# A fused model on one core: the gates of the experts moved ahead of the up matmul, in fp32, and spread by DMAs from DRAM

## The chip, the cores and the metric

The kernel runs on one core of one Trainium2 chip. The metric is the device time of one execution in microseconds, as the median of several runs. A core has TensorE (PE), VectorE (DVE), ScalarE (ACT), GpSimd (POOL) and SyncE (SP), each with its own queue of instructions; they order one another by semaphores, and SP and ScalarE issue DMAs.

## The reference

The whole model is computed in one launch: a mix of four geometric features into 64 channels, a state-space network of four layers, a mixture of experts, an attention and an LSTM, each with a layer norm ahead and a residual. There are 64 sequences of T = 96 tokens with 64 channels. The change is in the mixture of experts, with E = 16 experts, hidden width F = 128, the best K = 2 taken:

```python
gate_logits = x @ gate_w + gate_b
topk_vals, topk_idx = jax.lax.top_k(gate_logits, K)
topk_w = jax.nn.softmax(topk_vals, axis=-1)
h = jax.nn.relu(jnp.einsum('bsh,ehf->bsef', x, w1) + b1)
expert_out = jnp.einsum('bsef,efh->bseh', h, w2) + b2
sel = jnp.take_along_axis(expert_out, topk_idx[:, :, :, None], axis=2)
moe = jnp.sum(topk_w[..., None] * sel, axis=2)
y = x + moe
```

x is here a layer norm of h over its 64 channels, without scale and shift, so its channels sum to zero. A layer norm of y, with gamma and beta, follows. Everything is fp32.

## The kernel before

Every engine has its instructions written out in a block of its own, with explicit semaphores (`S("name")`); the order in the code is the order on the engine. Semaphores of the expert stage: `m_z` up, `m_r` relu, `m_g` gate spread, `m_h` product, `m_d` down, `m_mo` result out of PSUM.

The 6144 tokens stand as 12 groups `q` of 512 (NQ = 12). Every group passes all 16 experts, each weighted by its gate, which is zero for 14 of them. Experts go in pairs: the even one on partitions 0 to 63 of the 64-row operands, the odd one on 64 to 127. XD holds x with the channels on partitions, twice. There are 96 pairs, in six blocks `i` of 16 pairs `P` (two groups). For each pair:

- `up` (PE, line 1334): two fp32 matmuls of W1f with 512 tokens of XD into PSUM banks 0 to 3
- `weigh` (PE, line 1341): two bf16 matmuls of a 0/1 matrix `sel` with GP, the gates cut in three bf16 pieces, which give each expert's gate on all 128 partitions, in banks 4 and 5
- ACT, line 591: relu with the bias b1T into Rb; DVE, line 935: product of Rb and the gates in PSUM into Hb; one each for either expert
- `down` (PE, line 1326): two fp32 matmuls of w2s with Hb, summed over the experts in bank 6; ahead of a group's first, three bf16 matmuls add b2 times the gates (line 1324)

TensorE's order is up, weigh, down of the pair before. In the first block VectorE also computes the second part of the gates (`gate(1, k)`, 24 steps). In the other blocks the layer norm of the block before stands between the products (`settle`, in the pairs that the table SETTLE names), with GpSimd's powers and scaling, ScalarE's squares and copies, and TensorE's transposes (`sums_out`, `norm_out`). The gates are computed token-major on VectorE, turned by TensorE (`gates_turn`, line 1283) and copied out by ScalarE (`gates_out`, line 568). `xs_pe`, `xs_act` and `xs_dve` fill XD ahead of that. At the start of the program SP issues all loads in one order; GpSimd builds constants, `sel` among them, and prepares b2.

## Time and profile before

| | |
|---|---|
| median of 3 runs | 954.13 us (952.63 to 955.64) |
| the profiled execution | 950.02 us, span 947.5 us |
| PE busy | 772.4 us (82%) |
| DVE busy | 586.2 us (62%) |
| ACT busy | 393.7 us (42%) |
| POOL busy | 250.6 us (26%) |
| expert stage | 234.4 to about 488 us |
| DMA over the span | 10.21 MB, 11 GB/s mean |

Times of rows are from one profiled execution. In a timeline a row is: start in us, length in us, engine, line, operation, output<-inputs, shape, count; in brackets the idle time of the engine ahead of it and who ended it. In a group of instructions the two numbers after the bar are busy us and mean ns of one. An fp32 matmul of the program is recorded as two instructions, and two of them run side by side on the halves of the array. Lines are those of the kernel before.

### The profile page before, as it was taken

The numbers are of one execution on the slowest core, as the hardware profiler recorded it, in microseconds if no ns is written. First come the engines' busy times: TensorE is split into PE (matmuls) and PEld (weight loads), VectorE is DVE, ScalarE is ACT, GpSimd is POOL, SyncE is SP. The second block draws the span as 40 slices with busy tenths as digits, with TensorE's granted clock in tenths as the row PEclk, the third lists the DMA queues.
The fourth block names the chain that finished last, engine by engine and source line by source line (L and its number), as shares of the span: only waits on it lengthen the run. The fifth ranks groups of instructions, "written<-read, shape, count | busy, mean of one in ns | idle before, by whom it ended". The sixth has DMA issues, their size and how long they took to land.

```text
span 947.5 us, 17575 instructions
## 1 busy us (share of the span) xinstructions
PE 772.4 (82%) x6745; PEld 441.9 (47%) x6745; DVE 586.2 (62%) x1243; ACT 393.7 (42%) x791; POOL 250.6 (26%) x211
## 2 busy tenths in 40 slices
PE   3788888536999999999985777888999688888875
PEld 2675556425232222222223444565767555555554
DVE  4847655697766676676655655476776645545543
ACT  2233434233465565656541142344545233333332
POOL 8675555581001110202110302122233311001100
PEclk9988898755999999999986677799999955555555
DMA  9700000000000000000000000000000000000000
GB/s 190 126 8 1 1 1 1 1 0 1 1 1 1 1 1 1 1 1 1 1 0 1 1 1 1 2 1 2 1 1 2 1 7 10 10 10 10 10 10 12
DMA packets 23838, 10.21 MB, mean 11 GB/s; under 512 B 17414, under 2 KB 23574, under 8 KB 23766
## 3 DMA queue, kind: packets, MB, share of 16 engines
q1 hardware_dynamic: 22678, 8.92, 5.1%
q8 instruction: 54, 0.88, 0.4%
q10 hardware_dynamic: 1088, 0.26, 0.2%
q14 instruction: 18, 0.15, 0.1%
HBM read 7.60 MB, written 1.57 MB: 10 GB/s over the span
## 4 chain that ended last, share of the span: by engine, by line
PE 30%; DVE 11%; ACT 6%; issue 4%; POOL 1%; DVEq 0%; ACTq 0%; POOLq 0%
PE PS L1543 6%; PE PS L1398 3%; PE PS L1377 3%; PE PS L1447 3%; PE PS L1458 2%; PE PS L1419 2%; ACT LS L679 2%; ACT LS L675 2%; PE PS L1429 2%; DVE LS L1057 2%; DVE LS L1049 2%; DVE LS L1055 2%; PE PS L1326 1%; PE PS L1334 1%; DVE am L992 1%
## 5 line engine op out<-in xcount | busy, mean ns | idle before, releaser
L935 DVE TENSOR_TENSOR XC<-PS,Y 128x512 f32<-128x512 f32 x192 | 124.8, 686 | 80.9 <-ACT Y L591 80.7
L591 ACT ACTIVATE Y<-PS,b1T 128x512 f32<-128x512 f32 x192 | 121.2, 683 | 96.0 <-PE PS L1334 95.8
L1334 PE MATMUL PS<-XD,W1f 64*128 64x512 f32 x384 | 109.3, 646 | 1.6 <-ACT UF L568 1.6
L1543 PE MATMUL PS<-LS,V 64*64 64x32 f32 x1140 | 80.7, 294 | 34.7 <-DVE LS L1057 32.8
L1326 PE MATMUL PS<-XC,w2s 128*64 128x512 f32 x384 | 104.4, 622 | 1.9 <-DVE XC L935 1.9
L1543 PEld LDWEIGHTS PS<-LS,V 64*64 64x64 f32 x1140 | 67.9, 215 | 68.4 <-DVE LS L1057 66.7
L463 POOL TENSOR_TENSOR st<-st,mhalf 128x8 f32<-128x8 f32 x12 | 19.6, 1636 | 250.4 <-DVE st L918 250.4
L1334 PEld LDWEIGHTS PS<-XD,W1f 64*128 64x128 f32 x384 | 29.3, 186 | 66.4 <-ACT Y L591 50.3
L675 ACT ACTIVATE LS<-PS 128x64 f32<-128x64 f32 x96 | 21.4, 223 | 87.3 <-PE PS L1543 86.6
L1049 DVE SCALAR_TENSOR_TENSOR LS<-LS 128x32 f32<-128x32 f32 x96 | 19.6, 205 | 60.2 <-ACT LS L675 60.2
L1377 PE MATMUL PS<-BIG,MMs 64*128 64x512 f32 x96 | 37.0, 853 | 19.6 <-ACT EX L615 6.8
L175 POOL TENSOR_TENSOR st<-st,mhalf 128x8 f32<-128x8 f32 x24 | 39.3, 1637 | 47.0 <-DVE st L768 47.0
L1533 PE MATMUL PS<-XD,U 65*64 65x128 f32 x288 | 48.6, 439 | 0.8 <-ACT XD L669 0.8
L1341 PE MATMUL PS<-UF,sel 48*128 48x512 bf16 x192 | 37.2, 381 | 9.9 <-DVE XC L935 9.7
L494 POOL TENSOR_TENSOR st<-st,mhalf 128x8 f32<-128x8 f32 x6 | 9.8, 1636 | 126.8 <-DVE st L1041 126.8
L1178 PE MATMUL PS<-ident,UT 128*128 128x128 f32 x120 | 24.5, 339 | 21.1 <-POOL UT L177 21.0
L1447 PE MATMUL PS<-Y,UT 32*64 32x128 f32 (+2 forms) x768 | 35.7, 277 | 5.7 <-ACT XC L627 3.0
L992 DVE TENSOR_REDUCE am<-PS 128x8 f32<-128x768 f32 (+2 forms) x28 | 29.5, 1053 | 16.5 <-PE PS L1401 12.6
L482 POOL TENSOR_TENSOR Y<-Y,am 128x768 f32<-128x768 f32 (+1 forms) x10 | 16.4, 1644 | 85.0 <-DVE am L981 42.9
L1341 PEld LDWEIGHTS PS<-UF,sel 48*128 48x128 bf16 x192 | 9.4, 93 | 61.6 <-DVE XC L935 59.2
L1326 PEld LDWEIGHTS PS<-XC,w2s 128*64 128x64 f32 x384 | 19.0, 134 | 40.6 <-issue 37.8
L1057 DVE SCALAR_TENSOR_TENSOR LS<-LS 128x32 f32<-128x32 f32 x96 | 18.4, 192 | 28.3 <-ACT LS L679 28.3
(243 smaller groups left out, 1525.2 us busy)
## 6 DMA issues: line engine op xcount, KB each, us to landing
BIG<-in_x SPq DMA_DIRECT2D x8, 512.0 KB, 12.0
out<-X SPq DMA_DIRECT2D x48, 32.0 KB, 2.0
W1f<-in_L_ffn_w SPq DMA_DIRECT2D x2, 512.0 KB, 6.2
H<-in_txt SPq DMA_DIRECT2D x2, 256.0 KB, 12.3
w2s<-in_L_ffn_w SPq DMA_DIRECT2D x1, 512.0 KB, 6.1
BB<-in_L_attn_Bm ACTq DMA_DIRECT2D x2, 64.0 KB, 6.2
bds<-in_L_attn_Dm SPq DMA_DIRECT2D x2, 64.0 KB, 2.7
XD<-in_L_attn_Wq SPq DMA_DIRECT2D x1, 128.0 KB, 2.9
```

The costliest lines, as they stand in the source:

```text
L175: pool.tensor_tensor(st[:, 3, sj], st[:, 2, sj], mhalf[:, 0:KC * 2], ALU.pow).then_inc(S("s_r"), 1)
L591: act.activation(Rb[:, e % 4, :], PS[:, e % 4, :], ACT.Relu, bias=b1T[:, e:e + 1]).then_inc(S("m_r"), 1)
L675: act.activation(Tb[:, u % 2, 0:2 * HN], PS[:, 2 + par, 2 * HN * s:2 * HN * (s + 1)], ACT.Tanh).then_inc(S("l_t"), 1)
L935: dve.tensor_tensor(Hb[:, e % 4, :], PS[:, 4 + e % 2, :], Rb[:, e % 4, :], ALU.mult).then_inc(S("m_h"), 1)
L992: dve.tensor_reduce(stat_a(x, 0), scores(UNITS[x]), AX_X, ALU.max).then_inc(S("a_mx"), 1)
L1326: pe.matmul(PS[64 * (e % 2):64 * (e % 2) + 64, 6, :], w2s[:, e, :], Hb[:, e % 4, :], start=False, stop=(p == E - 2)).then_inc(S("m_d"), 1)
L1334: pe.matmul(PS[:, e % 4, :], W1f[r, e, :], XD[r, q * 512:(q + 1) * 512], start=True, stop=True).then_inc(S("m_z"), 1)
L1341: pe.matmul(PS[:, 4 + e % 2, :], sel[r, e, :], GP[r, q * 512:(q + 1) * 512], start=True, stop=True).then_inc(S("m_g"), 1)
L1377: pe.matmul(PS[:, 6 + h, :], MMs[p, half, :, :].rearrange("p a d -> p (a d)"), XAb[p, b0:b0 + GA, RB * r:RB * r + RB], start=True, stop=Tr ...
L1447: mm = pe.matmul(PS[64 * a:64 * a + 64, 4 + (JOBS[u] + k) % 2, x * 128:(x + 1) * 128], XT[p, u % 2, x, :], PT[p, u % 2, a, x, :], start=Tr ...
L1533: mm = pe.matmul(dst[64 * h:64 * h + 64], U3[:, g, :], xt[:, :, h, :], start=(g != 1), stop=(k == 0), skip_group_check=True)
L1543: mm = pe.matmul(PS[r, b, o:o + HN], V3[r, g, :], HB[r, (t - 1) % 4, :], start=False, stop=True, skip_group_check=True)
```

## The change

The gate now multiplies the input of an expert instead of its hidden values. This is right because relu(g z) = g relu(z) for g of zero or more, and g x W1 + g b1 = g (x W1 + b1). So that b1 needs no step of its own, row 0 of XD is set to one (scale 0 and bias 1 on that partition, by `zo`), row 0 of W1f becomes b1, and W1's row 0 is subtracted from the other rows (the channels of x sum to zero). The gate weights are treated likewise. The gates stay in fp32: turned by one transpose for each 16 columns (`gates_turn`), copied out (GT), written to a DRAM tensor gd, and read back by two DMAs for each pair, each of which reads one row of 512 gates for 64 partitions, into one of NS = 6 slots GB. VectorE multiplies XD by GB into Rb (`weigh`). The relu of a pair is ScalarE's for the even expert and VectorE's for the odd one. The gate matmuls (`weigh` on TensorE) go, and so do the b2 matmuls of each group: b2 times the gates is one fp32 matmul for each 1024 tokens (`bias_out`), added to X by VectorE (`bias_in`).

```diff
+        gw0 = sb("gw0", [128, E])
+        zo = sb("zo", [128, 2])
+        gd = nc.dram_tensor("gd", [NC, E, CH * 128], F32)
...
+        G2 = UT[:, :, :, :].rearrange("p k h d -> p (k h d)")[:, 0:NC * 128].rearrange("p (c e m) -> p c e m", c=NC, e=E)
+        GT = EX[:, 0:NC * 128].rearrange("p (c t) -> p c t", c=NC)
+        b2d = EX[:, 2048:2560].rearrange("p (m d) -> p m d", m=CH)
+        W10 = EX[:, 0:E * F].rearrange("p (e f) -> p e f", e=E)
+        NS = 6
+        GB = UF[:, :, :].rearrange("p k c -> p (k c)").rearrange("p (n c) -> p n c", n=NS)
...
-                    act.activation(XDp()[0:64, 4 * c:4 * c + 4, a, :], bank4(4 + c % 2)[64 * a:64 * a + 64], ACT.Copy).then_inc(S("xs_h"), 1)
...
+                    act.activation(XDp()[0:64, 4 * c:4 * c + 4, a, :], bank4(4 + c % 2)[64 * a:64 * a + 64], ACT.Identity,
+                                   bias=zo[0:64, 1:2], scale=zo[0:64, 0:1]).then_inc(S("xs_h"), 1)
...
-                    dve.tensor_copy(XDp()[64:128, 4 * c:4 * c + 4, a, :], bank4(4 + c % 2)[64 * a:64 * a + 64]).then_inc(S("xs_l"), 1)
...
+                    dve.tensor_scalar(XDp()[64:128, 4 * c:4 * c + 4, a, :], bank4(4 + c % 2)[64 * a:64 * a + 64], zo[64:128, 0:1], zo[64:128, 1:2],
+                                      ALU.mult, ALU.add).then_inc(S("xs_l"), 1)
...
-            sp.dma_start(b1s[:, :], b1).then_inc(S("ld_moe"), 16)
+            sp.dma_start(W10, w1[:, 0, :].rearrange("(a e) f -> a e f", a=1).to_broadcast([128, E, F])).then_inc(S("ld_w1"), 16)
+            sp.dma_start(gw0[:, :], gate_w[0:1, :].to_broadcast([128, E])).then_inc(S("ld_w1"), 16)
             sp.dma_start(w2s[:, :, :], w2.rearrange("e f h -> f e h")).then_inc(S("ld_moe"), 16)
-            for g in range(3):
-                sp.dma_start(b2f[E * g:E * g + E, 0, :], b2).then_inc(S("ld_moe"), 16)
+            sp.wait_ge(S("b2z"), 1)
+            for m in range(CH):
+                sp.dma_start(b2d[m:128:CH, m, :], b2).then_inc(S("ld_moe"), 16)
...
+            sp.wait_ge(S("w1c"), 2)
+            for h in range(2):
+                sp.dma_start(W1f[64 * h:64 * h + 1, :, :], b1.rearrange("(a e) f -> a e f", a=1)).then_inc(S("ld_b1"), 16)
+            def gates_write(c):
+                sp.wait_ge(S("g_t"), c + 1)
+                sp.dma_start(gd[c, :, :].rearrange("e t -> (e t)").rearrange("(p t) -> p t", p=128), GT[:, c, :]).then_inc(S("gdw"), 16)
+            def gates_spread(n):
+                if n >= NS:
+                    sp.wait_ge(S("m_x"), n - NS + 1)
+                q, p = n // (E // 2), n % (E // 2)
+                for h in range(2):
+                    sp.dma_start(GB[64 * h:64 * h + 64, n % NS, :],
+                                 gd[q // 2, 2 * p + h:2 * p + h + 1, q % 2 * 512:q % 2 * 512 + 512].to_broadcast([64, 512])).then_inc(S("gb%d" % (n % NS)), 16)
+            for n in range(NQ * E // 2):
+                if n == 0:
+                    gates_write(0)
+                    gates_write(1)
+                    sp.wait_ge(S("gdw"), 32)
+                if n == 22:
+                    for c in range(2, NC):
+                        gates_write(c)
+                if n == 2 * E:
+                    sp.wait_ge(S("gdw"), 16 * NC)
+                gates_spread(n)
...
-            seq(pool.memset(sel[:, :, :], 0.0), "sel")
-            for g in range(3):
-                for r in range(2):
-                    seq(pool.affine_select(out=sel[:, :, :], in_=sel[:, :, :], compare_op=ALU.not_equal, fill=1.0,
-                                       base=-E * g - 64 * r, pattern=[[-1, E], [0, F]], channel_multiplier=1), "sel")
+            seq(pool.memset(b2d, 0.0), "b2z")
+            for k in range(2):
+                seq(pool.memset(zo[:, k:k + 1], 1.0 - k), "zo")
+                for h in range(2):
+                    seq(pool.memset(zo[64 * h:64 * h + 1, k:k + 1], 1.0 * k), "zo")
...
-            pool.wait_ge(S("ld_moe"), 16 * 8)
-            seq(pool.memset(b2p[:, :, D:2 * D], 0.0), "b2z")
-            for i in range(3):
-                seq(pool.tensor_copy(b2p[:, i, 0:D], b2f[:, i % 2, :]), "b2c")
-                if i < 2:
-                    seq(pool.tensor_tensor(b2f[:, (i + 1) % 2, :], b2f[:, i % 2, :], b2p[:, i, 0:D], ALU.subtract), "b2c")
+            pool.wait_ge(S("ld_w1"), 16 * 6)
+            seq(pool.tensor_tensor(W1f[:, :, :], W1f[:, :, :], W10, ALU.subtract), "w1c")
+            seq(pool.tensor_tensor(GWs[:, :], GWs[:, :], gw0[:, :], ALU.subtract), "w1c")
...
-                act.wait_ge(S("gp_tp"), c + 1)
-                act.activation(GP[0:64 + 3 * E, c * CW:(c + 1) * CW], PSb[0:64 + 3 * E, gate_bank(c), :], ACT.Copy).then_inc(S("gp"), 1)
+                act.wait_ge(S("g_tp"), c + 1)
+                act.activation(GT[:, c, :], PS[:, gate_bank(c), 0:128], ACT.Copy).then_inc(S("g_t"), 1)
...
-                        act.activation(Rb[:, e % 4, :], PS[:, e % 4, :], ACT.Relu, bias=b1T[:, e:e + 1]).then_inc(S("m_r"), 1)
...
+                    n = i * E + P
+                    act.wait_ge(S("m_z"), n + 1)
+                    if n >= 2:
+                        act.wait_ge(S("m_d"), n - 1)
+                    act.activation(Hb[:, n % 2 * 2, :], PS[:, n % 2 * 2, :], ACT.Relu).then_inc(S("m_h"), 1)
...
-                    op = dve.tensor_tensor(LG, K1, K2, ALU.add)
-                elif k in (19, 21, 23):
-                    op = dve.tensor_copy(gp[:, :, (k - 19) // 2, :], (LG, SC, K1)[(k - 19) // 2])
-                elif k == 20:
-                    op = dve.tensor_tensor(SC, LG, gp[:, :, 0, :], ALU.subtract)
                 else:
-                    op = dve.tensor_tensor(K1, SC, gp[:, :, 1, :], ALU.subtract)
+                    ca, cb = a // CH, b // CH
+                    op = dve.tensor_tensor(G2[:, ca:cb, :, :].rearrange("p c e m -> p c m e"), K1.rearrange("p (c m) e -> p c m e", m=CH),
+                                           K2.rearrange("p (c m) e -> p c m e", m=CH), ALU.add)
...
+            def weigh(n):
+                q, p = n // (E // 2), n % (E // 2)
+                dve.wait_ge(S("gb%d" % (n % NS)), 32 * (n // NS + 1))
+                if n >= 4:
+                    dve.wait_ge(S("m_z"), n - 3)
+                dve.tensor_tensor(Rb[:, n % 4, :], XD[:, q * 512:(q + 1) * 512], GB[:, n % NS, :], ALU.mult).then_inc(S("m_x"), 1)
+            def bias_in(c):
+                dve.wait_ge(S("b2x"), c + 1)
+                xc = X[:, c * CH:(c + 1) * CH, :]
+                dve.tensor_tensor(xc, PS[:, gate_bank(c), :].rearrange("p (m d) -> p m d", d=D), xc, ALU.add).then_inc(S("b2a"), 1)
+            def relu(n):
+                dve.wait_ge(S("m_z"), n + 1)
+                if n >= 2:
+                    dve.wait_ge(S("m_d"), n - 1)
+                dve.tensor_scalar(Hb[:, n % 2 * 2 + 1, :], PS[:, n % 2 * 2 + 1, :], 0.0, None, ALU.max).then_inc(S("m_h1"), 1)
             def experts(i, first=False):
-                for qq in range(2):
-                    for e in range(E):
-                        n = i * 2 * E + qq * E + e
-                        dve.wait_ge(S("m_r"), n + 5)
-                        dve.wait_ge(S("m_g"), n + 1)
-                        dve.wait_ge(S("m_d"), n + 1)
-                        dve.tensor_tensor(Hb[:, e % 4, :], PS[:, 4 + e % 2, :], Rb[:, e % 4, :], ALU.mult).then_inc(S("m_h"), 1)
-                        step = qq * E + e
-                        if first and step < 12:
-                            gate(1, step + 1)
-                        if first and 14 <= step <= GOPS:
-                            gate(1, step - 1)
-                        if not first and e % 2:
-                            for k in SETTLE.get(step // 2, ()):
-                                settle(i - 1, k)
+                for P in range(E):
+                    n = i * E + P
+                    relu(n)
+                    if n + 2 < NQ * E // 2:
+                        weigh(n + 2)
+                    if first:
+                        if P == 0:
+                            bias_in(0)
+                            bias_in(1)
+                        for k in ((1, 2), (3, 4), (5, 6), (7, 8), (9, 10), (11, 12), (), (13, 14, 15), (16, 17), (18,))[P] if P < 10 else ():
+                            gate(1, k)
+                        if P >= 12:
+                            bias_in(P - 10)
...
+                pe.transpose(PS[:, gate_bank(c), 0:128], G2[:, c, :, :].rearrange("p e m -> p (e m)"), ident[:, :]).then_inc(S("g_tp"), 1)
+            def bias_out(c):
+                pe.wait_ge(S("g_t"), c + 1)
+                pe.matmul(PS[:, gate_bank(c), :], GT[:, c, :], b2d.rearrange("p m d -> p (m d)"), start=True, stop=True).then_inc(S("b2x"), 1)
...
-                if p == 0:
-                    pe.wait_ge(S("m_mo"), q + 2)
-                    for g in range(3):
-                        pe.matmul(PS[:, 6, :], b2p[:, g, :], GP[0:3 * E, q * 512:(q + 1) * 512], start=(g == 0), stop=False)
-                for e in (p, p + 1):
-                    pe.matmul(PS[64 * (e % 2):64 * (e % 2) + 64, 6, :], w2s[:, e, :], Hb[:, e % 4, :],
-                              start=False, stop=(p == E - 2)).then_inc(S("m_d"), 1)
...
+                p = n % (E // 2)
+                pe.wait_ge(S("m_x"), n + 1)
+                if n >= 2:
+                    pe.wait_ge(S("m_h"), n - 1)
+                    pe.wait_ge(S("m_h1"), n - 1)
+                for h in range(2):
+                    r = slice(64 * h, 64 * h + 64)
+                    mm = pe.matmul(PS[:, n % 2 * 2 + h, :], W1f[r, 2 * p + h, :], Rb[r, n % 4, :], start=True, stop=True)
+                mm.then_inc(S("m_z"), 1)
...
-            def weigh(n):
-                q, p = n // E, n % E
-                pe.wait_ge(S("m_h"), n + 4)
-                for e in (p, p + 1):
-                    r = slice(64 * (e % 2), 64 * (e % 2) + 3 * E)
-                    pe.matmul(PS[:, 4 + e % 2, :], sel[r, e, :], GP[r, q * 512:(q + 1) * 512], start=True, stop=True).then_inc(S("m_g"), 1)
...
                 up(n)
-                weigh(n)
                 if n:
-                    down(n - 2)
-                if i == 0 and P >= 12:
-                    if P == 12:
+                    down(n - 1)
+                if i == 0 and P >= 10:
+                    if P == 10:
                         pe.wait_ge(S("gchain"), gates_done(1, GOPS))
-                    gates_turn(P - 10)
+                    if P > 11:
+                        bias_out(P - 10)
+                    if P > 10 and P < 15:
+                        gates_turn(P - 9)
```

How the rows move. In each fence is what stands on the engine, before or after; XC is Hb, Y is Rb (or, in GpSimd's and norm rows, another part of the same buffers), UF is GP before and GB after, EX is GT.

TensorE in the second block before, where a group of tokens begins and then the transposes of `sums_out`:

```order
L1334 MATMUL PS<-XD,W1f 128x512 x2
L1341 MATMUL PS<-UF,sel 128x512 x2
L1324 MATMUL PS<-UF,b2p 128x512 x3
L1326 MATMUL PS<-XC,w2s 64x512 x2
L1334 MATMUL PS<-XD,W1f 128x512 x2
L1341 MATMUL PS<-UF,sel 128x512 x2
L1326 MATMUL PS<-XC,w2s 64x512 x2
L1308 MATMUL PS<-ident,BIG 128x128 x4
```

The same place after:

```order
L1383 MATMUL PS<-Y,W1f 128x512 x2
L1372 MATMUL PS<-XC,w2s 64x512 x2
L1383 MATMUL PS<-Y,W1f 128x512 x2
L1372 MATMUL PS<-XC,w2s 64x512 x2
L1354 MATMUL PS<-ident,BIG 128x128 x4
```

The rows L1341 and L1324 are gone; up (now L1383) reads Rb, and down (now L1372) follows it directly.

TensorE ahead of the first pair before:

```order
L1259 MATMUL PS<-GWs,XD 128x16 x16
L1269 MATMUL PS<-W3T 64x64 x8
L1274 MATMUL PS<-Wus,W3T 64x64 x8
L1283 MATMUL PS<-identb,UT 64x128 x32
L1334 MATMUL PS<-XD,W1f 128x512 x2
L1341 MATMUL PS<-UF,sel 128x512 x2
L1334 MATMUL PS<-XD,W1f 128x512 x2
```

And after:

```order
L1309 MATMUL PS<-GWs,XD 128x16 x16
L1319 MATMUL PS<-W3T 64x64 x8
L1324 MATMUL PS<-Wus,W3T 64x64 x8
L1330 MATMUL PS<-ident,UT 128x128 x2
L1334 MATMUL PS<-EX 128x512 x2
L1383 MATMUL PS<-Y,W1f 128x512 x4
L1372 MATMUL PS<-XC,w2s 64x512 x2
```

The 32 bf16 transposes of the first two chunks are two fp32 ones, with two b2 matmuls (L1334) behind them, and up now also waits for VectorE's product.

VectorE at the end of a block and the start of the next, before (L935 is the product, L923 the copy of the turned result):

```order
L915 TENSOR_REDUCE st<-Y 128x8
L918 TENSOR_SCALAR st<-st 128x8
L935 TENSOR_TENSOR XC<-PS,Y 128x512 x6
L923 TENSOR_SCALAR BIG<-PS 64x4x2x64 x2
L935 TENSOR_TENSOR XC<-PS,Y 128x512 x6
L897 TENSOR_TENSOR Y<-PS,X 128x256
L894 TENSOR_TENSOR Y<-PS,Y 128x256
```

And after (L973 is the relu of the odd expert, L962 the product of x and gates two pairs ahead):

```order
L944 TENSOR_REDUCE st<-Y 128x8
L947 TENSOR_SCALAR st<-st 128x8
L973 TENSOR_SCALAR XC<-PS 128x512
L962 TENSOR_TENSOR Y<-XD,UF 128x512
L973 TENSOR_SCALAR XC<-PS 128x512
L962 TENSOR_TENSOR Y<-XD,UF 128x512
L973 TENSOR_SCALAR XC<-PS 128x512
L962 TENSOR_TENSOR Y<-XD,UF 128x512
L952 TENSOR_SCALAR BIG<-PS 64x4x2x64 x2
L973 TENSOR_SCALAR XC<-PS 128x512
L962 TENSOR_TENSOR Y<-XD,UF 128x512
```

Two products a pair have become one relu and one product. SP's queue, which before had nothing between the load of beta and the stores of the output, has after it:

```order
L394 DMA bet<-in_L_ffn_beta 128x64
L399 DMA W1f<-in_L_ffn_b 1x2048 x2
L403 DMA gd<-EX 128x128 x2
L410 DMA UF<-gd 64x512 x44
L403 DMA gd<-EX 128x128 x4
L410 DMA UF<-gd 64x512 x148
```

The first row is beta's load, the second b1's; then come the gates of two chunks of 1024 tokens to DRAM, and the 192 loads of gates, with the other four chunks' stores ahead of the 45th.

## Rows read from the trace of the kernel before

**Rows 1.** Busy time by stretch; last: granted clock, DMA share, GB/s.

```profile
207.00:234.40 27.40, 18.54 (x176) 16.36 (x176) 21.54 (x42) 9.25 (x16) 9.47 (x4) 0.53 0.00 1
...
234.40:278.65 44.25, 41.32 (x226) 12.37 (x227) 31.20 (x55) 23.91 (x37) 0.00 (x0) 0.96 0.00 1
...
426.86:468.73 41.87, 40.00 (x180) 11.21 (x178) 28.81 (x48) 24.49 (x39) 6.62 (x6) 1.00 0.00 1
```

**Rows 2.** Groups of the block 426.86 to 468.73, costliest first.

```profile
L935 DVE TENSOR_TENSOR XC<-PS,Y 128x512 f32<-128x512 f32 x33 | 21.3, 686 | 12.6 <-ACT Y L591 12.6
...
L591 ACT ACTIVATE Y<-PS,b1T 128x512 f32<-128x512 f32 x33 | 20.9, 683 | 15.8 <-PE PS L1334 15.7
...
L1341 PE MATMUL PS<-UF,sel 48*128 48x512 bf16 x32 | 6.2, 379 | 1.9 <-DVE XC L935 1.9
...
L923 DVE TENSOR_SCALAR BIG<-PS 64x512 f32<-64x512 f32 x2 | 2.1, 1044 | 0.1
```

**Rows 3.** Timeline of TensorE in that stage: start, length, engine, line, operation.

```profile
420.00 1.13 PE L1334 MATMUL PS<-XD,W1f 64*128 64x512 f32 x4
420.97 0.38 PE L1341 MATMUL PS<-UF,sel 48*128 48x512 bf16 x2
421.28 1.08 PE L1326 MATMUL PS<-XC,w2s 128*64 128x512 f32 x4
422.29 1.13 PE L1334 MATMUL PS<-XD,W1f 64*128 64x512 f32 x4
...
426.86 1.13 PE L1334 MATMUL PS<-XD,W1f 64*128 64x512 f32 x4
...
428.05 0.81 PE L1324 MATMUL PS<-UF,b2p 48*128 48x512 bf16 x3
...
429.79 1.13 PE L1334 MATMUL PS<-XD,W1f 64*128 64x512 f32 x4
...
441.26 0.66 PE L1316 MATMUL PS<-ident,Y 128*128 128x128 f32 x4
441.84 1.13 PE L1334 MATMUL PS<-XD,W1f 64*128 64x512 f32 x4
```

**Rows 4.** Timeline of all engines before the first expert pair.

```profile
224.77 0.88 DVE L844 TENSOR_TENSOR Y<-Y,gs 128x256 f32<-128x256 f32 x2
...
231.46 0.27 ACT L561 ACTIVATE MMs<-PS 128x128 f32<-128x128 f32 x1
...
231.75 0.38 ACT L564 ACTIVATE NPt<-PS 64x256 f32<-64x256 f32 x1
...
232.15 1.94 ACT L568 ACTIVATE UF<-PS 112x1024 bf16<-112x1024 bf16 x2
...
234.42 1.13 PE L1334 MATMUL PS<-XD,W1f 64*128 64x512 f32 x4 [1.59 <-ACT UF L568]
```

**Rows 5.** DMA issues: KB each, median us from issue to landing.

```profile
XD<-in_L_attn_Wq SPq DMA_DIRECT2D x1, 128.0 KB, 2.9
...
out<-X SPq DMA_DIRECT2D x48, 32.0 KB, 2.0
...
gam<-in_L_ffn_gamma SPq DMA_DIRECT2D x1, 32.0 KB, 3.5
```

**Rows 6.** Timeline of SP's queue: the issue of one of them.

```profile
38.93 0.52 SPq L376 DMA_DIRECT2D XD<-in_L_attn_Wq  x1
```

**Rows 7.** Busy time by stretch, while x, Wk and then gamma, beta load.

```profile
7.00:12.00 5.00, 1.54 (x12) 1.31 (x12) 0.06 (x1) 1.00 (x2) 4.71 (x3) 1.00 1.14 211
...
41.80:42.00 0.20, 0.00 (x0) 0.00 (x0) 0.20 (x2) 0.08 (x1) 0.00 (x0) 1.00 1.06 369
...
52.40:53.40 1.00, 0.45 (x3) 0.04 (x1) 0.94 (x3) 0.74 (x2) 0.92 (x2) 0.50 0.08 22
```

**Rows 8.** Timeline of GpSimd ahead of the first layer.

```profile
60.86 6.72 POOL L453 TENSOR_TENSOR H<-H,boutr 128x3072 f32<-128x3072 f32 x1
...
79.94 1.67 POOL L175 TENSOR_TENSOR st<-st,mhalf 128x8 f32<-128x8 f32 x1 [12.36 <-DVE st L768]
```

## What I predict, and why

> **What bounds the kernel now.** I read the busy time by stretch first [rows 1]. The expert stage runs from 234.4 to about 488 us. In the block of 16 pairs from 426.86 to 468.73, which I take for all five behind the first, TensorE is busy 40.0 of 41.9 us at a granted clock of 1.00 (the 2.4 GHz level), VectorE 28.8, ScalarE 24.5, and the DMA engines do nothing. So TensorE sets this stage; a change is worth here what it takes off TensorE's row of work, as long as the others stay below it.
>
> The groups of the block say what the other engines do [rows 2]: ScalarE's relu 683 ns and VectorE's product 686 ns, 32 or 33 of each, TensorE's gate matmuls 379 ns, and only 1.9 us of the block is TensorE waiting for VectorE. TensorE's rows in order of time [rows 3] give the price of each step from start to start. Up matmuls start at 420.00, gate matmuls at 420.97, down matmuls at 421.28, the next up matmuls at 422.29. A pair is 0.97 + 0.31 + 1.01 = 2.29 us. The three b2 matmuls stretch a pair from 2.29 to 429.79 - 426.86 = 2.93, so 0.64 us, and four transposes take 0.58 (441.26 to 441.84). A block is then 16 x 2.29 + 2 x 0.64 + 3 x 0.58 = 39.7 us; the 2.2 us that are left of 41.87 are stalls.
>
> **The expert blocks.** The change takes the 192 gate matmuls (`weigh` on TensorE) and the 36 b2 matmuls away. What stays per pair is up and down: 0.97 + 1.01 = 1.98 us. The trace never shows up followed directly by down. At the least the gain is a third of the 0.64 us that three b2 matmuls of the same length cost, 0.21 (2.08 per pair), if the turn from up to down costs as much as the two turns do now; at the most it is 0.38, the length of a gate matmul (1.91). I take 0.31, since 0.97 is also what up takes where its successor is ready. A block: 16 x 1.98 + 3 x 0.58 + stalls. Of the 2.2 us of stalls I keep a third, 0.7, because a late VectorE step has now a slack that it has not today: relu of pair n is ready 1.13 + 0.69 = 1.8 us after up(n) starts, and down(n), behind up(n+1), is due at 1.98 + 0.97 = 2.95. That gives 34.1 against 41.87, so 7.8 less, five times: **-38.8 us**. With all 2.2 kept it is -31.
>
> VectorE covers this. Per pair it has a relu of the odd expert from PSUM and a product of two SBUF tiles. Neither stands in the trace; the nearest is the product from PSUM, 0.69 us, of which two take 1.29 in a row, so 0.60 each from start to start. A block is 16 x 1.20 + 7.5 (28.8 less 21.3, the layer norm steps) = 26.7 of 34.1 us. ScalarE has one relu a pair in place of two, and is no candidate. If the cover were gone (each operation at 0.9 us) VectorE would need 36 us a block, and set the pace there.
>
> **The first block.** It takes 44.25 us now. VectorE still has the second part of the gates in it: 13 or so long operations, two per pair, so 4 x 0.60 = 2.4 us in six or seven pairs in place of 1.98, and two additions of the b2 product in pair 0. 31.7 + about 3.7 for VectorE + four b2 matmuls of 128x512 at about 1.0 (nearest: a down pair, 1.01) + four turns at 0.15 to 0.3 = 40.3: **-4.0 us**.
>
> **The start of the stage.** Now the last of TensorE's results before it leaves ScalarE at 232.13, two evictions of 0.97 follow, and up starts at 234.42 [rows 4]. After: two products (0.88) move behind the last x copy, so ScalarE is free at 231.3. Two evictions of 128x128 at 0.27 end at 231.8. Then two things are new and stand on the path: the gates are written to DRAM, and only then read back. A store of 32 KB lands 2.0 us after issue, a load of 64 rows of 2 KB (Wq) 2.9, and its issue takes the queue 0.52 [rows 5, 6]. 231.8 + 0.1 + 2.0 = 233.9; + 0.52 + 2.9 = 237.4; product 0.69 and two handovers: up at 238.2, **+3.8 us**. The granted clock is 0.53 ahead of the stage and 0.96 in its first block [rows 1]: TensorE enters it at the lower level either way, so the longer wait gets no term of its own. The Trainium skill (DMA: Bandwidth & Descriptors, Bandwidth) has about 2.0 us plus bytes over 436 GB/s for one DMA, 2.3 us for these 128 KB where the trace has 2.9; by it the term would be +3.2.
>
> **The spread itself.** Each pair needs two DMAs of 128 KB, 96 pairs, all reading one row of 2 KB 64 times. SP: 2 x 0.52 = 1.04 us of issue in 2.13 us a pair, six pairs ahead; covered. The transfer: 262 KB in 2.13 us is 123 GB/s. How fast can it go? [rows 7] Loads of different pieces of 1 KB (x) with a full queue: 211 GB/s. Rows of 2 KB (Wk): 369 GB/s in the 0.2 us in which they pass. But the two broadcasts of the trace, gamma and beta, 256 B read by 128 partitions each, crawl: 22 GB/s, flat for over 2 us, at an 8% share of the engines. So the engines are not short of anything; the one place that all read from is. That is the number on which this prediction hangs. If what limits is the 256 B piece, a row of 2 KB is eight such places: 8 x 22 = 176 GB/s, 1.49 us a pair, hidden below 2.13. If the whole row is one such place, it is 22 GB/s. I take the first, since distinct pieces have run at 211 and 369 in this trace and only identical ones at 22; the traces do not show a row of several pieces read by all.
>
> **Before the stage.** W10 is a broadcast of 1 MB in the load queue, over 16 rows of 512 B, 5 us at 211 GB/s. GpSimd gets a subtraction of 128x2048, 2048/3072 of the 6.72 us that the addition of 128x3072 takes, 4.5 us, and that addition is queued behind it; it ends now at 67.6, and GpSimd is next wanted at 79.94 [rows 8]. 12.4 us of slack hide 4.5 and a queue that ends some 5 us later: 0. At 22 GB/s W10 takes 48 us, the loads of the LSTM weights behind it arrive near 93, and with 13 us of GpSimd's work the layers would start at 106: +26. The x copies with a scale and a bias in place of plain ones I take at the same time.
>
> **Sum.** Against the profiled execution's own 950.02 us (span 947.5): -38.8 - 4.0 + 3.8 = -39.0, 911. The median of the three runs, 954.13, is 4.1 above it, and that is what a median is compared with: 915.
>
> **The rivals.**
> 1. *The source of the spread is the bound, and the kernel gets slower.* All 16 engines read the same row; the 22 GB/s row speaks for it, the 8% share too, the 369 GB/s against. Below 100 GB/s (262 KB in today's 2.62 us a pair) it decides. With four places per row, 88 GB/s: 2.98 us a pair, 286 us in place of 254 plus the start: 950 + 32 + 4 = 986, chance 0.12; that is the version on the slower side by a few per cent. With one or two, 22 or 44 GB/s: 11.9 or 5.96 a pair, 1144 or 572 us in place of 254: 1845 or 1270, chance 0.13.
> 2. *The spread reaches half of the 211 GB/s.* 105 GB/s, 2.49 us a pair, 239 in place of 254: about 940, and with a late start no change. Chance 0.12. The Trainium skill (DMA: Bandwidth & Descriptors, Latency and other measured facts) reports streams that walk through HBM in step at one large power-of-two pitch at 103 where others had 214 GB/s, and infers aliasing of channels; readers of one row are in step by construction. That halving of 211 is this rival; the flat 22 here is worse than the page's case.
> 3. *VectorE or the handovers set the pace* and most of the stalls stay. 26.7 of 34.1 us speaks against, the doubled steps at a block's end (two of 1.04 us beside 1.2) for it. About 925. Chance 0.13, counted within the forecast's 0.63, in whose range it lies.
>
> **How the numbers follow.** Forecast 0.63, own range 903 to 937: 1.91 or 2.08 us a pair is -7 or +10, stalls kept +8, start +-2. Rival 2 0.12, rival 1 0.12 and 0.13. From 903 to 990 leaves out the 0.13 and a few hundredths below. Faster by over 0.3% (about what a measurement here can tell from none): 0.63 and half of rival 2, 0.69; within 0.3%: 0.05; slower: 0.26.
>
> **What would show it.** Right: up starts 1.98 us apart in most pairs of a block, no wait for UF's transfers after the first, DMA near 123 GB/s through the stage, up(0) near 238, blocks of 34 us, everything before 200 us in place. Wrong: VectorE's products wait for DMAs each pair (the spacing then gives the rate of the spread: 2.98 is 88 GB/s); or up to down takes over 1.07; or VectorE late in each pair; or the first layer starts after 80 us.

## The result and the profile after

The kernel after takes 923.27 us (median, 921.92 to 927.37); the kernel before, run beside it, 953.38. The ratio is 0.968 (0.963 to 0.973; it holds a fifth execution of after, 917.70): 30 us faster, with a forecast of 915 and a range of 903 to 990. The profiled execution of after is the longest of its four, 927.37 (span 925.4).

The stage first, by the busy time in three stretches that answer to [rows 1]: ahead of the first pair, its block, and a later block.

```profile
215.80:243.29 27.49, 18.25 (x130) 13.78 (x131) 17.71 (x29) 8.18 (x15) 5.50 (x1) 0.54 0.09 25
243.29:283.83 40.54, 38.69 (x136) 9.95 (x137) 33.69 (x56) 11.49 (x22) 0.00 (x0) 0.96 0.45 141
354.93:390.59 35.66, 35.04 (x142) 9.29 (x140) 29.31 (x48) 14.02 (x23) 6.95 (x5) 1.00 0.35 118
```

A block takes 35.66 us where it took 41.87, and TensorE is busy 35.04 of them: it still sets the stage. The DMA engines, idle before, now move 118 GB/s at a 0.35 share. The groups of that last block answer to [rows 2]:

```profile
L1383 PE MATMUL PS<-Y,W1f 64*128 64x512 f32 x64 | 18.1, 641 | 0.0
L1372 PE MATMUL PS<-XC,w2s 128*64 128x512 f32 x66 | 17.9, 616 | 0.2 <-DVE XC L973 0.2
L962 DVE TENSOR_TENSOR Y<-XD,UF 128x512 f32<-128x512 f32 x17 | 12.2, 721 | 0.0
L973 DVE TENSOR_SCALAR XC<-PS 128x512 f32<-128x512 f32 x16 | 11.0, 690 | 4.4 <-PE PS L1383 4.3
L630 ACT ACTIVATE XC<-PS 128x512 f32<-128x512 f32 x16 | 9.6, 597 | 19.2 <-PE PS L1383 19.2
```

TensorE waits 0.2 us for VectorE, and VectorE's product has no wait for its DMA. TensorE's timeline at the end of the block before it answers to [rows 3]:

```profile
347.61 1.13 PE L1383 MATMUL PS<-Y,W1f 64*128 64x512 f32 x4
348.67 1.08 PE L1372 MATMUL PS<-XC,w2s 128*64 128x512 f32 x4
349.68 1.13 PE L1383 MATMUL PS<-Y,W1f 64*128 64x512 f32 x4
...
352.27 0.66 PE L1362 MATMUL PS<-ident,Y 128*128 128x128 f32 x4 [0.46 <-POOL Y L505]
352.86 1.13 PE L1383 MATMUL PS<-Y,W1f 64*128 64x512 f32 x4
```

Up to down is 1.06 us, down to up 1.01: a pair is 2.07 us. The start of the stage, all engines, answers to [rows 4]:

```profile
235.52 0.69 PE L1330 MATMUL PS<-ident,UT 128*128 128x128 f32 x2
235.62 0.28 ACT L597 ACTIVATE MMs<-PS 128x128 f32<-128x128 f32 x1 [6.17 <-PE PS L1324]
...
236.75 0.45 ACT L604 ACTIVATE EX<-PS 128x128 f32<-128x128 f32 x2
237.05 0.83 SPq L403 DMA_DIRECT2D gd<-EX  x2
...
239.10 6.86 SPq L410 DMA_DIRECT2D UF<-gd  x11
242.46 0.69 DVE L962 TENSOR_TENSOR Y<-XD,UF 128x512 f32<-128x512 f32 x1 [7.62 <-DMA UF<-gd]
243.29 1.13 PE L1383 MATMUL PS<-Y,W1f 64*128 64x512 f32 x4 [2.37 <-DVE Y L962]
```

The gates leave ScalarE at 237.20 and the first pair starts at 243.29, 6.1 us later. Next, GpSimd and VectorE at the start of the layers, which answer to [rows 8]:

```profile
66.45 0.25 POOL L481 TENSOR_SCALAR b<-b 128x12 f32<-128x12 f32 x1 [12.03 <-DMA V<-in_L_ffn_V_o]
...
68.45 4.52 POOL L483 TENSOR_TENSOR W1f<-W1f,EX 128x2048 f32<-128x2048 f32 x1
...
73.34 6.66 POOL L488 TENSOR_TENSOR H<-H,boutr 128x3072 f32<-128x3072 f32 x1
83.98 1.67 POOL L176 TENSOR_TENSOR st<-st,mhalf 128x8 f32<-128x8 f32 x1 [3.98 <-DVE st L804]
```

```profile
73.53 7.03 DVE L813 TENSOR_TENSOR Y<-Y,UT 128x512 f32<-128x512 f32 x1 [3.36 <-ACT Y L577]
...
81.92 0.68 DVE L813 TENSOR_TENSOR Y<-Y,UT 128x512 f32<-128x512 f32 x1
```

GpSimd's first power of the layers comes at 83.98 in place of 79.94. The row to look at is VectorE's: one product of 128x512 takes 7.03 us where the next of its kind takes 0.68, and it ends 0.56 us after GpSimd's addition (80.00). TensorE was early there (its matmuls of L1217 began at 67.90, those of the same step before the change, L1165, at 70.18), so more than the 4.0 us was lost.

Why GpSimd's work starts so late stands in SP's queue: the landing of W10, the issue of the eight b2 loads, and the last load of the queue, after and then before.

```profile
EX<-in_L_ffn_w SPq DMA_DIRECT2D x1, 1024.0 KB, 14.9
```

```profile
40.97 11.65 SPq L382 DMA_DIRECT2D EX<-in_L_ffn_b  x8
...
66.04 0.43 SPq L394 DMA_DIRECT2D bet<-in_L_ffn_beta  x1
```

```profile
51.01 0.43 SPq L385 DMA_DIRECT2D bet<-in_L_ffn_beta  x1
```

From the traces of before and after: 4.0 us lost ahead of the layers, 4.8 from there to the first pair, 34.6 gained between the first pair and the first attention queries (255.85 to 221.24). The rest, whose code did not change, took 457.2 before and 460.9 here. In the other executions profiled below it took 452.5 to 457.2, so differences of single spans under 5 us say nothing; stages are compared instead. The runs below were made in three series, each beside runs of the kernel before (median 952.85, 953.51 and 954.31 us).

### The profile page after: what moved, and what is told of

Same layout as the page of the kernel before. It is cut to its first block, busy times and chain, and to the rows that moved or that the text cites. A ratio compares the mean times of both kernels' runs of the same rounds, so it can differ in the third digit from the quotient of the medians.

```text
span 925.4 us, 17120 instructions
## 1 busy us (share of the span) xinstructions
PE 754.5 (82%) x6438; PEld 435.8 (47%) x6438; DVE 591.8 (64%) x1236; ACT 328.9 (36%) x695; POOL 234.2 (25%) x207
## 4 chain that ended last, share of the span: by engine, by line
PE 46%; DVE 29%; ACT 8%; issue 7%; POOL 7%; DMA 1%; ACTq 0%; SPq 0%; DVEq 0%; POOLq 0%
PE PS L1583 6%; PE PS L1383 5%; PE PS L1372 5%; PE PS L1438 4%; PE PS L1487 3%; PE PS L1417 3%; PE PS L1498 3%; ACT LS L717 2%; PE PS L1459 2%; ACT LS L713 2%; DVE Y L962 2%; POOL st L499 2%; PE PS L1469 2%; DVE XC L819 2%; DVE LS L1109 2%
## 5 line engine op out<-in xcount | busy, mean ns | idle before, releaser
L1383 PE MATMUL PS<-Y,W1f 64*128 64x512 f32 x384 | 109.3, 646 | 2.8 <-DVE Y L962 2.8
L1372 PE MATMUL PS<-XC,w2s 128*64 128x512 f32 x384 | 104.0, 619 | 2.8 <-DVE XC L973 2.0
L630 ACT ACTIVATE XC<-PS 128x512 f32<-128x512 f32 x96 | 57.3, 597 | 124.8 <-PE PS L1383 124.7
L973 DVE TENSOR_SCALAR XC<-PS 128x512 f32<-128x512 f32 x96 | 66.2, 689 | 27.3 <-PE PS L1383 27.0
L962 DVE TENSOR_TENSOR Y<-XD,UF 128x512 f32<-128x512 f32 x96 | 68.2, 710 | 8.6 <-DMA UF<-gd 8.6
L1383 PEld LDWEIGHTS PS<-Y,W1f 64*128 64x128 f32 x384 | 29.1, 186 | 70.5 <-issue 49.0
L1372 PEld LDWEIGHTS PS<-XC,w2s 128*64 128x64 f32 x384 | 19.4, 135 | 76.9 <-issue 72.2
L1417 PE MATMUL PS<-BIG,MMs 64*128 64x512 f32 x96 | 34.6, 802 | 17.8 <-ACT EX L653 6.0
L1487 PE MATMUL PS<-Y,UT 32*64 32x128 f32 (+2 forms) x768 | 38.1, 295 | 5.9 <-ACT XC L665 3.1
L1487 PEld LDWEIGHTS PS<-Y,UT 32*64 32x64 f32 (+2 forms) x768 | 30.1, 144 | 8.4 <-ACT XC L665 4.4
## 6 DMA issues: line engine op xcount, KB each, us to landing
EX<-in_L_ffn_w SPq DMA_DIRECT2D x1, 1024.0 KB, 14.9
```

What stands on the lines that cost most here:

```text
L630: act.activation(Hb[:, n % 2 * 2, :], PS[:, n % 2 * 2, :], ACT.Relu).then_inc(S("m_h"), 1)
L962: dve.tensor_tensor(Rb[:, n % 4, :], XD[:, q * 512:(q + 1) * 512], GB[:, n % NS, :], ALU.mult).then_inc(S("m_x"), 1)
L973: dve.tensor_scalar(Hb[:, n % 2 * 2 + 1, :], PS[:, n % 2 * 2 + 1, :], 0.0, None, ALU.max).then_inc(S("m_h1"), 1)
L1372: mm = pe.matmul(PS[64 * h:64 * h + 64, 6, :], w2s[:, 2 * p + h, :], Hb[:, n % 2 * 2 + h, :], start=(p == 0), stop=(p == E // 2 - 1))
L1383: mm = pe.matmul(PS[:, n % 2 * 2 + h, :], W1f[r, 2 * p + h, :], Rb[r, n % 4, :], start=True, stop=True)
L1417: pe.matmul(PS[:, 6 + h, :], MMs[p, half, :, :].rearrange("p a d -> p (a d)"), XAb[p, b0:b0 + GA, RB * r:RB * r + RB], start=True, stop=Tr ...
```

## The experiments

**1. GpSimd's work off the start of the layers.** Why does one product take 7 us? The first run moves only the subtraction:

```diff
-            pool.wait_ge(S("ld_w1"), 16 * 6)
-            seq(pool.tensor_tensor(W1f[:, :, :], W1f[:, :, :], W10, ALU.subtract), "w1c")
-            seq(pool.tensor_tensor(GWs[:, :], GWs[:, :], gw0[:, :], ALU.subtract), "w1c")
...
                 for j in range(NJ):
                     ssm_scale(pool, l, j)
+            pool.wait_ge(S("ld_w1"), 16 * 6)
+            seq(pool.tensor_tensor(W1f[:, :, :], W1f[:, :, :], W10, ALU.subtract), "w1c")
+            seq(pool.tensor_tensor(GWs[:, :], GWs[:, :], gw0[:, :], ALU.subtract), "w1c")
```

> GpSimd's subtraction of W10 from W1f moves behind the four layers; the loads stay as they are. Theory (GpSimd holds VectorE): VectorE's first product of the layers, 7.03 us long in the kernel after beside GpSimd's addition of 128x3072 (73.34 to 80.00), was started at 73.53 and could not run until that addition ended. Here the addition starts at about 68.5 and ends at 75.1, so the product ends at about 75.7, and GpSimd's first power of the layers starts at about 78.6 in place of 83.98: 5.4 us less, 918 against 923. The subtraction costs nothing in its new place, since GpSimd idles 12.5 us between the layers and the layer norm. Rival (the 7.03 us were something else, such as late data or one slow instruction): the product stays near 7 us wherever GpSimd's addition ends, and the time stays at 923. The Trainium skill (SBUF - State Buffer, practical consequences) says that a VectorE instruction with two SBUF inputs and a GpSimd one that reads SBUF lock each other out for a whole instruction; by it the theory holds.

Measured: 914.76 us (913.21 to 919.61), ratio to before 0.961 (0.954 to 0.967). GpSimd, then VectorE:

```profile
67.53 6.68 POOL L485 TENSOR_TENSOR H<-H,boutr 128x3072 f32<-128x3072 f32 x1
78.18 1.67 POOL L176 TENSOR_TENSOR st<-st,mhalf 128x8 f32<-128x8 f32 x1 [3.98 <-DVE st L804]
```

```profile
71.92 2.83 DVE L813 TENSOR_TENSOR Y<-Y,UT 128x512 f32<-128x512 f32 x1 [3.36 <-ACT Y L577]
```

The addition ends at 74.21, the product at 74.75: again 0.54 us behind it, whatever its own start. So the product's length is set by the end of GpSimd's operation, and the rival falls. The first power comes at 78.18, 5.8 us sooner than in the kernel after.

That it takes two operands from SBUF is seen in the second profile of the kernel after (experiment 8). There GpSimd subtracts from 70.01 to 74.52 and adds from 75.22 to 81.88. VectorE beside it:

```profile
71.85 3.21 DVE L813 TENSOR_TENSOR Y<-Y,UT 128x512 f32<-128x512 f32 x1 [3.36 <-ACT Y L577]
75.09 0.69 DVE L817 TENSOR_REDUCE st<-Y 128x8 f32<-128x512 f32 x1
75.81 6.61 DVE L819 SCALAR_TENSOR_TENSOR XC<-st,Y 128x512 f32<-128x512 f32 x1
```

The two operations with two SBUF operands end 0.54 us behind the subtraction and behind the addition. The reduction between them, with one, takes its 0.69 us, 0.56 of it beside the addition. The Trainium skill (SBUF — State Buffer, Who interferes with whom) says that a VectorE instruction with two SBUF inputs and a GpSimd one that reads SBUF exclude each other for the whole instruction. The rows of GpSimd's additions and subtractions agree. Its power of 128x8 does not: in the kernel after, a product of VectorE ran from 339.00 in 0.68 us inside the power's 338.50 to 340.14 (the spans of GpSimd's instructions are rough).

The second run also moves the loads of W10, gw0 and b2d behind all others.

```diff
-            sp.dma_start(W10, w1[:, 0, :].rearrange("(a e) f -> a e f", a=1).to_broadcast([128, E, F])).then_inc(S("ld_w1"), 16)
...
             for t, v, n in ((gbr, gate_b, E), (gam, gamma, D), (bet, beta, D)):
                 sp.dma_start(t[:, :], v.rearrange("(a n) -> a n", a=1).to_broadcast([128, n])).then_inc(S("ld_moe"), 16)
+            sp.dma_start(W10, w1[:, 0, :].rearrange("(a e) f -> a e f", a=1).to_broadcast([128, E, F])).then_inc(S("ld_w1"), 16)
...
```

> As the run before it, and the loads of W10, gw0 and of the eight b2 pieces are issued behind all others. Theory: GpSimd no longer waits for the LSTM weights until 66.45 (they land near 53, as before the change), its addition of 128x3072 ends before 62, the product takes 0.69 us, and GpSimd's first power starts at 77.7, 6.3 us less than after and 2.3 less than in the kernel before: 917 against 923. Rival (TensorE or VectorE are late themselves ahead of the layers): no more than 4 us come back, since 4.0 is what the layers start later than in the kernel before.

Measured: 914.99 us (912.5 to 917.83), ratio 0.960 (0.954 to 0.966). The addition runs from 56.01 to 62.73, the product takes 0.69, the first power comes at 76.68 and the first pair at 235.44 (237.78 in the run before it). So 7.3 us come back at the layers, 5.8 of them without moving a load; the 1.5 us between the two runs do not show in their medians. Beside their own runs of the kernel before, these two save 38 us, where the kernel after saved 30. That is 8 us more and within the spread of the medians of the 5.8 and 7.3 of the traces.

**2. How fast can the gates be spread?** This was the number on which the forecast hung. The gates are loaded twice, the second time into unused places, and the product waits for both.

```diff
                     sp.dma_start(GB[64 * h:64 * h + 64, n % NS, :],
...
+                    sp.dma_start(G9[n % NS][64 * h:64 * h + 64, :],
+                                 gd[q // 2, 2 * p + h:2 * p + h + 1, q % 2 * 512:q % 2 * 512 + 512].to_broadcast([64, 512])).then_inc(S("gb%d" % (n % NS)), 16)
```

> Each load of gates is issued twice, the second into unused places, and the product waits for both: 524 KB for each pair, 253 GB/s at 2.07 us a pair; SP issues four DMAs a pair, about 4 x 0.45 = 1.8 us. Theory A (one row read by 64 partitions is no special source, the engines give over 250 GB/s): the time grows by less than 5 us, blocks stay near 35.7. Theory B (the source row is a hot place and gives 8 x 22 = 176 GB/s): 2.98 us a pair, 96 x 0.91 = 87 us more, about 1010. Theory C (somewhere between, the 211 GB/s of the x loads): 2.48 us a pair, 40 us more, about 963. DMA GB/s in the stage gives the ceiling in B and C.

Measured: 958.19 us (954.14 to 961.73), ratio 1.004 (1.001 to 1.007): nearest to theory C. But SP's rows and the stretch 340 to 400 us point to another limit than the transfer:

```profile
342.34 0.60 SPq L413 DMA_DIRECT2D EX<-gd  x1
342.97 0.60 SPq L411 DMA_DIRECT2D UF<-gd  x1
```

```profile
340.00:400.00 60.00, 52.78 (x208) 13.94 (x204) 41.43 (x69) 19.60 (x32) 8.27 (x7) 1.00 0.66 199
```

An issue each 0.64 us without a gap is 2.56 us a pair and 131 KB / 0.64 = 205 GB/s, and a DMA landed 3.2 us after issue, hardly later than the 2.8 of the kernel after. Two more runs were made on this. In the first, one DMA brings both rows of a pair, 256 KB, and a second one their copy.

```diff
+                two = gd[q // 2, 2 * p:2 * p + 2, q % 2 * 512:q % 2 * 512 + 512].unsqueeze(1).to_broadcast([2, 64, 512])
+                sp.dma_start(GB[:, n % NS, :], two).then_inc(S("gb%d" % (n % NS)), 16)
+                sp.dma_start(G9[n % NS][:, :], two).then_inc(S("gb%d" % (n % NS)), 16)
```

> The gates are again loaded twice, as in the run with the spread issued twice (200 GB/s, SP issuing without a gap at 0.64 us each, 3.2 us from issue to landing), but each DMA now brings both rows of a pair to 128 partitions, 256 KB: half as many issues for the same bytes. Theory (SP's issues were the limit at 200 GB/s, not the rows that are read): the pair falls back to 2.1 us, the stage moves 250 GB/s, and the time is 923 to 935. Rival (the transfer was the limit): 2.6 us a pair, 200 GB/s and 958 as before.

Measured: 1691.47 us (one execution). Neither theory: the edit brought a limit of its own. The stretch 500 to 600 us:

```profile
500.00:600.00 100.00, 39.24 (x82) 8.22 (x80) 17.20 (x27) 9.83 (x15) 6.63 (x5) 0.50 0.13 51
```

A share of 0.13 is two of 16 engines, and each issue took 5.00 us, in which its 262 KB went at 52 GB/s. The outermost dimension of this access is 2, where it was 64. The Trainium skill (DMA: Bandwidth & Descriptors, Rules for kernel authors) says that an outermost dimension of c < 16, a broadcast among them, confines a DMA to at most c engines; the row agrees. As a test of the issues this run is void.

In the second, DMAs and bytes stay as in the run with the spread issued twice, but ScalarE issues the second copy.

```diff
                     act.activation(Hb[:, n % 2 * 2, :], PS[:, n % 2 * 2, :], ACT.Relu).then_inc(S("m_h"), 1)
+                    second(n + 4)
```

> The gates are loaded twice as in the run with the spread issued twice (SP alone, 0.64 us from issue to issue, 200 GB/s, 2.6 us a pair, 958), but ScalarE issues the second copy, two DMAs after its relu in each pair; rows, bytes and rows per DMA are the same. Theory (SP's issues were the limit): the stage moves about 250 GB/s, a pair takes 2.1 us, 925 to 935. Rival (the transfer, two rows read 128 times each in a pair and a copy of each, was the limit): 200 GB/s and 958 again. Second rival (ScalarE's issues, 2 x 0.6 us beside a relu of 0.6 us, pace the pair): 2.1 to 2.3 us a pair with waits of TensorE for ScalarE.

Measured: 933.89 us (one execution). The stretch 340 to 400 us:

```profile
340.00:400.00 60.00, 57.43 (x230) 15.09 (x228) 49.81 (x78) 24.04 (x37) 13.92 (x10) 1.00 0.80 229
```

Pairs are back at 2.07 us (a block takes 36.5), TensorE has no wait for VectorE's product in a block, and 229 GB/s pass, landing after 3.8 us. So one queue was the limit at 200, and the rows read give at least 229. Their true ceiling was not reached. Whether SP's issuing or what the queue does behind it set the 0.64 us was not separated: the run with half the issues would have told.

**3. What a broadcast costs by itself.** Eleven loads, one at a time, in the kernel after; the one of 512 B:

```diff
+            sp.dma_start(BIG[:, 128:256], w1f[0:128].rearrange("(a n) -> a n", a=1).to_broadcast([128, 128])).then_inc(S("pr"), 16)
+            pr(3)
```

> The kernel after with eleven loads added, one at a time, in the stretch between 60 and 230 us in which SP does nothing; the time should stay within 3 us of 923. Each is read from the DMA's own transfer time: one row of 256 B, 512 B, 1 KB, 2 KB, 4 KB and 8 KB to 128 partitions, distinct rows of 256 B, 2 KB and 4 KB, sixteen strided pieces of 512 B to all partitions (as W10), and one row of 2 KB to 64 partitions. Theory of the prediction (the 256 B place limits, so that a longer row is more places): 22 GB/s at 256 B, 44 at 512 B, 88 at 1 KB, 176 at 2 KB, then the ceiling of distinct rows. Rival (identical rows are nothing special, and the short piece is slow by itself): distinct rows of 256 B run at 22 GB/s too. Rival (one row is one place): 22 GB/s at every length, against which the kernel's own 123 GB/s speaks already.

Measured: 920.11 us (one execution, each load once), within the 3 us expected. In order: to all partitions a row of 256 B; distinct rows of 256 B; a row of 512 B, 1 KB, 2 KB; distinct rows of 2 KB; a row of 4 KB; distinct rows of 4 KB; a row of 8 KB; W10's sixteen pieces; last 2 KB to 64 partitions. The stretch of each; share and GB/s at the end:

```profile
74.40:76.90 2.50, 2.50 (x17) 1.56 (x16) 2.46 (x2) 0.00 (x0) 2.50 (x1) 1.00 0.07 20
77.90:78.50 0.60, 0.60 (x4) 0.00 (x0) 0.60 (x1) 0.00 (x0) 0.60 (x1) 1.00 0.24 55
79.70:81.30 1.60, 0.00 (x0) 0.00 (x0) 1.60 (x2) 0.07 (x1) 0.95 (x1) 0.87 0.17 40
82.40:84.10 1.70, 1.70 (x8) 1.70 (x8) 1.44 (x4) 0.00 (x0) 0.92 (x1) 0.50 0.26 77
85.30:87.30 2.00, 2.00 (x8) 0.72 (x4) 1.93 (x4) 0.26 (x1) 1.76 (x2) 0.50 0.55 131
88.50:90.20 1.70, 1.19 (x18) 1.02 (x20) 1.63 (x4) 0.56 (x2) 1.44 (x2) 1.00 0.52 154
90.90:93.40 2.50, 1.37 (x8) 1.04 (x10) 2.33 (x6) 1.19 (x3) 2.20 (x2) 0.54 0.57 210
94.70:97.00 2.30, 1.94 (x16) 1.61 (x18) 1.73 (x4) 0.46 (x1) 1.95 (x3) 0.50 0.75 228
98.00:101.60 3.60, 3.60 (x28) 3.23 (x27) 0.21 (x1) 0.60 (x1) 2.70 (x3) 0.53 0.83 291
103.30:115.70 12.40, 12.04 (x91) 6.86 (x92) 7.33 (x13) 5.51 (x9) 3.16 (x3) 1.00 0.41 85
117.30:118.40 1.10, 0.37 (x3) 0.37 (x4) 1.06 (x3) 0.79 (x2) 0.83 (x2) 1.00 0.31 119
```

Read the lengths, which hold some 0.2 us of margin: 128 reads of one row take 1.6 to 2.5 us from 256 B to 4 KB, so the rate grows with the row: 20, 40, 77, 131, 210 GB/s. 128 distinct rows of 256 B take 0.6 at most. So it is not the short piece by itself that is slow but reading the same one again, and the rate grows with the row as the forecast took it to. At 2 KB, the gates' size, identical rows take 2.0 us and distinct ones 1.7, and from 4 KB on they hardly differ (2.5 and 2.3). That the reason is one place of 256 B, and a longer row several of them, is not shown: a price for each repeated read, whatever its length, gives the same lengths. W10 speaks against places: sixteen rows of 512 B would be 32 of them, and it went at only 85 GB/s. The piece of 512 B alone is not the reason either, since the kernel before moved 207 GB/s from 31 to 35 us, nearly all of it distinct pieces of 512 B (W1f and w2s). Why W10 is slow was not found.

**4. The turn between up and down.** TensorE's order only:

```diff
+                if n % 2:
                     up(n)
+                    if n + 1 < NQ * E // 2:
+                        up(n + 1)
                     down(n - 1)
+                else:
+                    if n:
+                        down(n - 1)
```

> Only TensorE's order changes: up(n), up(n+1), down(n-1), down(n) in place of up, down, up, down, so that a turn between up and down comes once a pair in place of twice. Theory (what kept the pair at 2.07 us and not 1.98 is the turn between the two kinds of matmul: up takes 1.06 us when down follows it): a kind that follows itself starts 0.85 to 0.90 us later, a pair takes 1.89 to 1.95 us and a block 32.8 to 33.8 in place of 35.7, so 11 to 17 us less, about 909. Rival 1 (up costs 1.06 and down 1.01 whatever stands behind them): 2.07 us a pair, 923. Rival 2 (the relu comes late for a down that is moved nearer to it): TensorE waits for VectorE in every second pair, 923 or more.

Measured: 921.37 us (919.76 to 923.1), ratio 0.967 (0.963 to 0.970). TensorE in the second block:

```profile
297.88 1.99 PE L1383 MATMUL PS<-Y,W1f 64*128 64x512 f32 x8
299.80 1.94 PE L1372 MATMUL PS<-XC,w2s 128*64 128x512 f32 x8
301.67 1.99 PE L1383 MATMUL PS<-Y,W1f 64*128 64x512 f32 x8
...
305.46 1.13 PE L1383 MATMUL PS<-Y,W1f 64*128 64x512 f32 x4
307.78 1.13 PE L1383 MATMUL PS<-Y,W1f 64*128 64x512 f32 x4 [1.20 <-DVE Y L962]
```

Two pairs take 3.79 us, 1.89 each. Up follows up, and down follows down, after 0.86 us (1.99 - 1.13, 1.94 - 1.08); with a turn it is 1.06 and 1.01. So the turn theory holds, at 0.15 to 0.20 us a turn, two of them in a pair of 2.07. The Trainium skill (TensorEngine Tiling (Array Packing), Key Properties) has a change of tiling mode drain the engine; up is split by rows and down by columns, and the rows fit that, but it gives no price. No run separates the split from the other differences between up and down. The block stays at 35.36 us all the same (343.15 to 378.51): two waits for VectorE's product, 1.2 and 0.95 us, take most of the 16 x 0.18 = 2.9. So rival 2 is right about the block, though it is the product that is late, not the relu. In the median (921.37 against 923.27) nothing shows that is clear of the spread.

**5. The relu split.** Both relus on ScalarE, and VectorE's `relu(n)` taken out:

```diff
+                    act.activation(Hb[:, n % 2 * 2 + 1, :], PS[:, n % 2 * 2 + 1, :], ACT.Relu).then_inc(S("m_h1"), 1)
```

> The relu of the odd expert goes back to ScalarE; VectorE has only the product of a pair. Theory (VectorE sets the pace only in the five or six pairs of 2.52 us of the first block, and ScalarE has room for two relus of 0.53 us each in 2.07): pairs 2 to 6 of the first block fall to 2.1 us, 2 us less; at the end of the other blocks ScalarE's two copies of 2.15 us delay two relus, up to 1 us more in each of five. About the same time, 920 to 926. Rival (VectorE's relu is what keeps the blocks at 35.7 in place of 33.1 + 1.7): a block of 34.5 and less, 917.

Measured: 920.9 us (919.2 to 925.04), ratio 0.966 (0.962 to 0.971). The first block falls from 40.54 to 38.46 us, since VectorE's four operations a pair no longer pace it. The others grow a little, as expected: from 35.43 to 35.63 the second, from 35.67 to 35.97 the next three, and from 38.28 to 39.15 the last with its end. Together that gives 2.0 of the 2.1 us back: 221.1 us from the first pair to the first attention queries, where the kernel after has 221.2. The split of the relu is worth nothing here, in either direction.

**6. Grouped order with both relus on ScalarE,** the edits of 4 and 5 together.

> The grouped order of TensorE (1.89 us a pair where nothing waits, but 921 in all, since TensorE waited 1.2 and 0.95 us in each block for VectorE's products) together with both relus on ScalarE (920.9 alone). Theory (the grouped order pays as soon as VectorE is no longer in step with TensorE, so that its product can run ahead): blocks of 32.5 to 33 us in place of 35.6, the first one 37; 903 to 908. Rival (the product is late because of the layer norm step that waits for GpSimd, 1.17 us, whoever does the relus): blocks near 35, 918.

Measured: 915.74 us (915.25 to 917.56), ratio 0.960 (0.958 to 0.963). The gain is 7.6 us to the kernel after in the same series, and the theory is half wrong: up to the start of up(17), behind the first block's last down, it takes 38.96 us where the kernel after takes 42.61, and the later blocks still 35.44. VectorE where a product is late:

```profile
337.82 0.69 DVE L931 TENSOR_TENSOR H<-H,Y 128x512 f32<-128x512 f32 x1 [3.40 <-POOL Y L509]
338.54 0.69 DVE L963 TENSOR_TENSOR Y<-XD,UF 128x512 f32<-128x512 f32 x1
```

VectorE waits 3.40 us for GpSimd's scaling with gamma, with the next product queued behind. TensorE waits 1.09 us for it there, and 1.26 for GpSimd (L505) ahead of `norm_out`, where the kernel after has 0.46. So the rival holds for the blocks: the layer norm of the block before, whose steps stand at fixed pairs, does not shrink with the pairs. Moving its steps was not tried.

**7. The turn of the gates ahead of the small products.** On TensorE, and `gates_out` likewise on ScalarE:

```diff
+            for c in range(2):
+                gates_turn(c)
             pe.wait_ge(S("W3T"), 2)
...
-            for c in range(2):
-                gates_turn(c)
```

> TensorE turns the gates of chunks 0 and 1, and ScalarE copies them out, ahead of the 16 small products for the attention and their four evictions. Theory (the way of the gates through DRAM, 237.05 to 242.46, is the path to the first pair, so all that stands ahead of it counts): the first store is issued about 2 us earlier and up(0) starts 2 us earlier against the last transpose of x: 921. Rival (the last step of the gates on VectorE ends no earlier than the small products): no change.

Measured: 920.38 us (918.71 to 922.62), ratio 0.966 (0.962 to 0.969). From GpSimd's first power to the first pair it is 157.66 us where the kernel after has 159.31, 1.7 less; the theory holds, a little below its 2. The other runs that spread the gates once took 158.8 to 160.9, so the sign is clear and the size is not; the median cannot tell the run from the kernel after.

**8. All together** (the edits of 1, 4, 5 and 7), **and the kernel after once more.**

> All of it: the subtraction and the loads of W10 and b2 later (7.3 us at the first layer), the gates turned early (2.3 us at the first pair), grouped order, both relus on ScalarE. If the parts add up: 903 to 908 less 7 to 8 and less 2 to 3, so 892 to 899. Rival (parts of it are given back in the attention and LSTM, where the granted clock differs from run to run): the expert stage shows the whole gain, the median less of it.

> The kernel after once more, on the same chip as the three others and beside the same runs of the kernel before: 920 to 927.

Measured: 907.9 us (905.77 to 915.98), ratio 0.954 (0.950 to 0.957), for all; 923.37 (918.83 to 928.21), ratio 0.969 (0.965 to 0.973), for the kernel after. All together is 15.5 us faster than the kernel after and 46 faster than the one before. The parts add up in the trace. Against the first profile of the kernel after, the layers start 6.6 us sooner (77.37), the first pair comes 2.1 us sooner after that (234.56), and from there to the first queries it is 216.1 us, 5.1 less (216.9 in the grouped run of 6). Together that is 13.9. It misses the 892 to 899 by 9 to 16 us, nearly the 8 to 13 by which the run of 6 missed its own forecast: the later blocks, which grouped order was to shorten to 32.5 or 33 us, take 35.4 here too.

## Why the prediction was right or wrong

- **The direction and the bound: right.** TensorE set the stage and still does, and taking its gate matmuls away shortened it.
- **The expert blocks, -38.8: mis-sized, -31.** The blocks take 35.66 us, not 34.1. The term that failed is "what stays per pair is up and down: 0.97 + 1.01". The 0.97 was up followed by a gate matmul. Followed by down it is 1.06; with no turn behind it, it would be 0.86. 16 times the missing 0.09 is 1.4 us a block, 7 us in all. The step named this itself as its low bound of gain (2.08 us a pair). That the -31 also stands in the prediction, for all 2.2 us of stalls kept, is a coincidence. The stalls, kept at 0.7, were right: 35.66 - 16 x 2.07 - 1.74 leaves 0.8, of which 0.46 is the wait for GpSimd's L505.
- **The first block, -4.0: right,** 44.25 to 40.54, so -3.7. VectorE's pairs of 2.52 us are there, and went when the relu was moved.
- **The start of the stage, +3.8: +4.8.** The way through DRAM was right: 6.4 us forecast from ScalarE's last copy to the first pair, 6.1 measured. The rest lies ahead of it: the four evictions for the attention still stood before the gates' copies, and the turn put forward gave 1.7 us back. The prediction's estimate from the Trainium skill, 2.3 us for a load, comes from a fit for DMAs that GpSimd issues; these, issued by SP, landed after 2.8 us.
- **The spread itself, hidden: right.** The rate does grow with the row, and it leaves at least 229 GB/s against a need of 123. The stated reason, places of 256 B, fits one row of any length up to 2 KB but is not shown, and W10 does not fit it. Rivals 1 and 2 fall; rival 3's 925 came near, but its mechanism shows only in the first block.
- **Before the stage, 0: wrong, +4.0.** The step that failed is "12.4 us of slack hide 4.5 and a queue that ends some 5 us later". W10 took 14.9 us to land, not 5. The eight b2 loads took 11.65 us of issue and were not costed; 7.23 of them are the first one's, which stood behind W10 and w2s, and the three b2 loads of the kernel before took 4.83 in all. The queue ended 15 us later, and GpSimd, which waits for the loads behind, ended its addition at 80.00 in place of 67.6. The slack was counted to GpSimd's own next operation; what was hurt was VectorE, whose product could not run beside GpSimd's addition. That accounts for all of it: with both moved the layers start 3.3 us earlier than before the change. The prediction's own sign of being wrong, a first layer after 80 us, had come.
- **The sum.** 915 was 8.3 us too fast. The stages of the two traces miss by more, 13.2 us: 8.2 from the six blocks (7 of them the turns), 4.0 from ahead of the layers, 1.0 from the start. The stages give 4.0 + 4.8 - 34.6 = -25.8 us, and the medians fell by 30.1. The 4.3 us between them stand in no changed stage, and in the profiled pair the unchanged rest is 3.7 us longer, not shorter. (The kernel before was also 0.7 us faster here than the 954.13 it is counted from.) So it is luck that 915 missed by 8 us and not by 13, and where those 4 us come from stays open.

## What to carry to other kernels

- The price of a matmul is that of a neighbourhood: read it where the same kind of operation follows, and where none does, take the bound with the turn in it.
- Slack of GpSimd is not slack if VectorE reads two SBUF operands meanwhile (7.03 us for a product of 0.68): look at what both run in the same microseconds, not only at when GpSimd is wanted next.
- A kernel that takes TensorE's work away soon meets the next chain: here the layer norm of the block before, at fixed pairs, which kept a block at 35.4 us with pairs of 1.89.

## What the runs showed of the hardware that was not expected

- 128 reads of one DRAM row took 1.6 to 2.5 us whether the row had 256 B or 4 KB; 128 distinct rows of 256 B took under 0.6.
- A two-row broadcast with the rows as outermost dimension went at 51 GB/s over two engines' worth of share (0.13), against 199 GB/s from the same queue for the same bytes with 64 outermost.
- SP issued DMAs of 64 rows at best each 0.64 us while the engines were at a share of 0.66; this, not the rows read, capped one queue at 200 GB/s, since a second queue brought 229.
- VectorE's products go with longer GpSimd operations as well, where they start first: the addition of 128x3072 took 6.99 us in the run with the eleven loads, where a product had begun 0.23 us before it, and 6.66 in the kernel after. The power of 128x8 took 2.01 us in the run of 5, where one had begun 0.17 us before it, and 1.64 in the kernel after.
- A VectorE reduction of one SBUF operand kept its 0.69 us beside GpSimd's addition; a product and a SCALAR_TENSOR_TENSOR with two ended 0.54 to 0.56 us after GpSimd did, whatever their start.
